# Lists' work one turn later, and the third segment product ahead of the third projection

## What is computed

```python
h = qw[input]                                         # table rounded per row
zxbcdt = layernorm(h) @ in_proj_w.T                   # 1030 columns: z, xBC, dt
xBC = silu(conv4(xBC) + conv_b); dt = softplus(dt + dt_bias)
y = ssd(x * dt, dt * A, B, C) + D * x                 # 6 heads, one chunk of 128
y = rms(y * silu(z)) * norm_w
h = h + sigmoid(gate1) * (y @ out_proj_w.T) + layernorm(h)
# experts on n = layernorm(h): 4 common, 4 unique, top 1 by softmax
common  = gelu(n @ W1c[e] + b1c[e]) @ W2c[e] + b2c[e]
dropped = rank of the token within its common expert >= 2048
out = h + common + dropped * unique
```

## Time and profile before

| | |
|---|---|
| median of 3 runs | 1068.1 us (1067.28 to 1074.15) |
| the profiled run, device time | 1069.56 us |
| its span, first to last instruction | 1067.8 us |
| TensorE busy | 922.9 us, 86% |
| VectorE busy | 678.0 us, 63% |
| ScalarE busy | 583.9 us, 55% |
| GpSimd busy | 531.8 us, 50% |
| sequence stage, convolution of turn 1 to that of turn 16 | 32 to 553 us |
| first unit's hidden product | 612.8 us |

### The profile page before, as it was taken

The page is one execution under the profiler, slowest core; times in us unless marked ns, Lnnn a source line. Parts: engine busy times, 40 slices in busy tenths (PEclk is TensorE's granted clock), DMA queues, the critical chain, the costliest instruction groups (busy, mean ns, idle before and its releaser), DMA issues.

```text
span 1067.8 us, 19889 instructions
## 1 busy us (share of the span) xinstructions
PE 922.9 (86%) x5743; PEld 600.0 (56%) x5744; DVE 678.0 (63%) x1999; ACT 583.9 (55%) x1196; POOL 531.8 (50%) x638
## 2 busy tenths in 40 slices
PE   0678899888988988899989788899988999999985
PEld 0233455455544554555455556677776676767774
DVE  3678999898898988989879614566671221212120
ACT  3657887787768877887685344323332323233330
POOL 6322436356354373561523517443437777775452
PEclk9899999999899999999898789999998999999997
DMA  4910011011101110110000122123431212222220
GB/s 111 319 51 9 16 46 44 4 47 46 46 3 45 46 48 1 47 46 31 3 31 31 49 62 80 49 80 116 139 88 45 70 49 66 56 62 74 69 58 22
DMA packets 50001, 61.54 MB, mean 58 GB/s; under 512 B 22524, under 2 KB 41688, under 8 KB 49412
## 3 DMA queue, kind: packets, MB, share of 16 engines
q0 software_dynamic: 16704, 30.54, 9.9%
q1 hardware_dynamic: 28580, 24.93, 7.7%
q10 hardware_dynamic: 4640, 5.13, 1.6%
HBM read 36.24 MB, written 25.92 MB: 58 GB/s over the span
## 4 chain that ended last, share of the span: by engine, by line
PE 39%; DVE 25%; ACT 13%; issue 12%; POOL 8%; DMA 2%; DVEq 0%; ACTq 0%; POOLq 0%
DVE xbc L1432 9%; PE cx L1217 6%; PE yb L1217 5%; PE mm L1205 4%; PE mm L1201 4%; PE mm L1055 4%; PE mm L1059 3%; PE sg L1201 3%; POOL list_c L537 3%; POOL list_u L573 2%; DVE mix L1452 2%; ACT rows_s L745 2%; DMA xg<-hr_dram,ids 2%; ACT h L692 2%; PE sg L973 2%
## 5 line engine op out<-in xcount | busy, mean ns | idle before, releaser
L1432 DVE SCALAR_TENSOR_TENSOR xbc<-mm,cw,xbc 128x508 f32<-128x508 f32 (+2 forms) x231 | 168.5, 740 | 32.0 <-ACT xbc L720 26.5
L1055 PE MATMUL mm<-xt_a,win_a 128*128 128x512 f32 x248 | 142.7, 658 | 36.5 <-DVE xbc L1432 27.1
L901 ACT ACTIVATE ht<-mm,b1s 128x256 f32<-128x256 f32 x102 | 44.7, 472 | 222.3 <-PE sg L1205 219.7
L512 POOL TENSOR_TENSOR ybuf<-ybuf,zs 128x384 f32<-128x384 f32 x64 | 68.7, 1073 | 108.7 <-DVE ybuf L1465 108.5
L589 POOL DMA_INDIRECT xg<-hr_dram,ids x80 | 81.1, 1013 | 80.5 <-DVE res L1759 44.8
L608 POOL DMA_INDIRECT out_dram<-osb,ids_s x80 | 82.3, 1028 | 64.2 <-DVE osb L1769 44.9
L720 ACT ACTIVATE xbc<-mm,cb,cw 128x512 f32<-128x512 f32 x77 | 56.6, 775 | 102.2 <-PE mm L1059 102.2
L1769 DVE TENSOR_TENSOR osb<-cx,res 128x192 f32<-128x192 f32 x40 | 14.2, 356 | 128.4 <-PE cx L1217 119.1
L1201 PE MATMUL mm<-fx_a,w1a_t 128*128 128x256 f32 x240 | 81.7, 423 | 13.7 <-issue 7.6
L1205 PE MATMUL mm<-fx_b,w1b_t 64*128 64x256 f32 x240 | 85.2, 436 | 0.0
L1205 PE MATMUL sg<-fx_b,w1b_t 64*128 64x256 f32 x240 | 85.2, 436 | 0.0
(11 more groups left out here) (275 smaller groups left out, 2051.2 us busy)
## 6 DMA issues: line engine op xcount, KB each, us to landing
hr_dram<-hr SPq DMA_DIRECT2D x16, 768.0 KB, 3.5
w2s<-in_w2c_dram SPq DMA_DIRECT2D x4, 576.0 KB, 8.6
w2s_u<-in_w2u_dram ACTq DMA_DIRECT2D x4, 576.0 KB
list_c<-fill SPq DMA_DIRECT2D x2, 1032.0 KB, 12.3
list_u<-fill SPq DMA_DIRECT2D x2, 1032.0 KB, 18.4
w1a<-in_w1c_dram SPq DMA_DIRECT2D x4, 384.0 KB, 7.1
w1a_u<-in_w1u_dram ACTq DMA_DIRECT2D x4, 384.0 KB
xg<-hr_dram,ids POOLq DMA_INDIRECT x80, 3.1
```

The costliest lines, as they stand in the source:

```text
L1055: mmul(tile_bank(g2, m)[:, :], win_a[:, column(m):column(m) + P], xt_a[:, p, :], start=True, stop=False)
L1432: ins = stt(out=dst_[:, :, back:L], in0=src[:, :, 0:L - back], scalar=cw[:, m, TAPS - 1 - back:TAPS - back], in1=dst_[:, :, back:L], op0=A ...
```

## The change

`list_tokens`, `prefixes` and `places` now work on `listed_turn(t)`, the batch of group t - 5, so they run in the following turn: prefixes behind `seg(1)` and ahead of `y(0)`, places behind VectorE's `y(0)`, and the list writes in two halves, the first behind `gate_y(0)`, the second behind `norm2`. The third segment product `seg(2)` stands ahead of `project(2)`. KNOWN is 5, not 6, and `early_units` stands at the end of turn 16. In turn 17 GpSimd gathers the first two units first of all, and the transposes, the copy and the weights of unit 0 are done within that turn. SyncE stores the group of turn 17 behind the first loads of unit numbers.

```diff
-KNOWN = 6
+KNOWN = 5
+def listed_turn(t):
+    g = t - 5 if t <= LAST_SSD else t - 4
+    return (batch(g), g) if 0 <= g < NG else (None, None)
 # SyncE, experts_sp
+            sp.wait_ge(s_mm, (XT + ZT) * NG)
             turn(0, 0, 0, body)
+            store(LAST_SSD, *groups(LAST_SSD))
             store(NG + 2, *groups(NG + 2))
 # GpSimd
-                def list_tokens():
+                def list_tokens(part=None):
...
-                    for j in range(GS * (g5 + 1 - first)):
+                    for j in range(n) if part is None else range(part * n // 2, (part + 1) * n // 2):
...
                 if t == LAST_SSD:
+                    for p in range(2):
+                        pool.wait_ge(s_st[p], CREDIT + 16 * (KNOWN - p))
+                    pool.wait_ge(s_mm, (XT + ZT) * NG)
+                    for v in range(2):
+                        gather_unit(0, 0, v, 0)
                     gate_y(0)
                     gate_y(1)
                     rms()
-                    for p in range(2):
-                        pool.wait_ge(s_st[p], CREDIT + 16 * (KNOWN - p))
-                    gather_unit(0, 0, 0, 0)
                     gate_y(2)
                     gate_y(3)
                     norm2()
-                    gather_unit(0, 0, 1, 0)
+                    list_tokens()
                     return
                 gate_y(0)
+                list_tokens(0)
                 rms()
...
                 norm2()
+                list_tokens(1)
                 gate_y(3)
-                list_tokens()
 # ScalarE, turn 17
                     copy_side()
+                    copy_x(0)
 # TensorE, turn 17
                     seg(1)
+                    prefixes()
                     cbx(1)
...
                     side_back()
+                    transpose_x(0, 0)
                     out_product(0)
 # TensorE, turns 1 to 16
                 seg(1)
+                prefixes()
                 y(0)
                 cbx(1)
+                seg(2)
 
                 project(2)
                 to_tp(g5, 2, 0)
                 project(3)
                 to_tp(g5, 2, 1)
-                seg(2)
                 y(1)
...
                 project(7)
                 y(3)
-                prefixes()
 # VectorE, turn 17
-                    early_units()
                     weights(0)
                     weights(1)
+                    places()
...
                     weights(3)
+                    dve.wait_ge(s_wc, n_w)
+                    dve.wait_ge(s_early, 1)
+                    unit_weights(0, 0, 0, 0)
                     residual(0)
 # VectorE, turns 1 to 16
                 y(0)
+                places()
...
                     clip(t + 1)
-                places()
+                if t + 1 == LAST_SSD:
+                    early_units()
```

More of the change, by code:

```diff
@@ L875, in body, with copy_x @@
                 sum_rows()
+            def copy_x(unit):
+                act.wait_ge(f_t, unit + 1)
+                nc.scalar.copy(fx_a[:, :], tp[:, 0:TL])
+                for n in range(2):
+                    last = nc.scalar.copy(fx_b[n * DB:(n + 1) * DB, :], tp[0:DB, TL:2 * TL])
+                last.then_inc(f_x, 1)
             rounded(0)
@@ L883, in _ @@
             before = [0]
-            def copy_x(unit):
-                act.wait_ge(f_t, unit + 1)
-                nc.scalar.copy(fx_a[:, :], tp[:, 0:TL])
-                for n in range(2):
-                    last = nc.scalar.copy(fx_b[n * DB:(n + 1) * DB, :], tp[0:DB, TL:2 * TL])
-                last.then_inc(f_x, 1)
             def gelus(m, i, v, unit):
```

69 lines of the change are left out of this document (34 added, 35 removed).

## The result

| | before | changed |
|---|---|---|
| median beside each other | 1071.12 us (1067.28 to 1076.56, 4 runs) | 1054.93 us (1053.1 to 1062.65, 4 runs) |
| ratio of the two | | 0.9855, 95% interval 0.9812 to 0.9897 |
| the same, measured again later | 1071.64 us (16 runs) | 1059.34 us (1053.63 to 1062.65, 6 runs), ratio 0.9878, 0.9838 to 0.9918 |
| span of the profiled execution | 1067.8 us | 1051.3 us |

The change makes the kernel 1.2 to 1.5% faster; the forecast was 1052, between 1045 and 1061. Where the 16.5 us of the two profiled executions lie can be read from the start of conv(0) in each turn: at the conv(0) of turn 5 the changed kernel is 1.9 us ahead, at that of turn 16 12.0 us, at the end 16.5. So turns 5 to 15 give 10.1 us (388.8 to 378.7), what stands ahead of turn 5 1.9, and all that stands behind turn 15 4.5.

The account below looks back on a forecast made before the run. GpSimd's list writes were taken to bound following turns, VectorE batch turns. Gains of 16.8 + 0.5 + 4.7 = 22.0 us, less 3 for the clock and 3 for hand-offs, left 16: 1068.1 - 16 = 1052, range 1045 to 1061.

Parts of the forecast that it names:

- Following turns held by norm1: Following turns: norm1 behind GpSimd's list writes holds project(5); without that a turn takes 33.3 us, 2.1 less than turn 11.
- Batch turns: VectorE bounds batch turns; places leaving takes 0.56 us off 35.30, and 34.8 us was taken.
- Front of a following turn: conv(0) to conv(2) takes 7.7 us, with project(3) 0.1 late and places fitting into VectorE's 0.66 us wait.
- Middle and end of the turn: Following turn: conv(2) to ScalarE's read of project(5) takes 6.7 us, from there to the next conv(0) 18.9.
- seg(2): Moving TensorE's seg(2) ahead of project(2) is worth nothing; bounds for a turn -0.5 to +0.3 us.
- The second half of the writes: Four GpSimd writes, 5.3 us, delay gate_y(3); covered by 1.9 us before squares, so they cost nothing.
- Turn 15: Turn 15 rounds no further group on ScalarE and takes about 31.5 us.
- Turns 5 to 15 as a sum: These turns fall from 388.8 to 372.0 us, a gain of 16.8, before 3 us put back for low-clock stretches.
- hand-offs: Some twenty hand-offs in the sum were rounded down by 0.15 us, so 3 us were put back.
- Ahead of turn 5: Turn 4 adds a gain of 0.5 us.
- The transition: Turn 17: unit 0's hidden product no longer waits for its weights; gain 4.7 us, bounds 3 to 5.2.
- rival (d): Clock falls between seg(1) and y(0) in each following turn; at 6 us a turn, 14 slower: 1082; chance 0.05.

Follow-up runs that it names:

- Experiment 1: Kernel before, with GpSimd's norm1 of the next group ahead of the eight list writes instead of behind them: 1067.95 us, ratio 0.9991.
- experiment 4: Changed kernel with the first four list writes ahead of gate_y(0) on GpSimd instead of behind it: 1050.09 us, ratio 0.982.
- experiment 5: Changed kernel with seg(2) back behind the second half of to_tp: 1055.08 us, ratio 0.9845.
- experiment 9: Changed kernel with all eight list writes behind norm2, none behind gate_y(0): 1073.89 us, ratio 0.9995.
- experiment 7: Changed kernel with turn 17's prefixes ahead of seg(0) instead of behind seg(1): 1057.59 us, ratio 0.9887.
- experiment 6: Changed kernel with the transition undone (both gathers, unit 0's transposes, copy and weights at their old places): 1057.4 us without one run of 4883, ratio 0.9898.
- experiment 3: Changed kernel with following turns' prefixes issued twice: 1084.88 us, ratio 1.0119; with three dense products instead of the second set: 1064.01 us, ratio 0.993.
- experiment 2: Kernel of experiment 1 plus two dense products in TensorE's idle time ahead of the prefixes in each batch turn: 1057.0 us, ratio 0.9874.
- experiment 8: Kernel of experiment 4 plus six dense products in TensorE's waits ahead of seg(0) and seg(1) in turn 17: 1048.81 us, ratio 0.9793.
- experiment 10: Kernel of experiment 8 with the last four VectorE operations of pick moved to the end of the following turn: 1052.58 us, ratio 0.9815.

## Why the prediction held, and where it did not

**Following turns held by norm1: right.** Experiment 1 shows it by itself: 33.6 us instead of 35.4.

**Batch turns: right.** 34.7, with 34.8 forecast.

**Front of a following turn: 7.7 forecast, 8.10 measured.** The term that was mis-sized is places: 0.56 us from the end of a batch turn, where nothing ran beside it, and 1.26 us at its new place beside gate_y(0). Both stood in the order shown ahead of the prediction, y(0) releasing gate_y(0) and places following y(0), and I priced places by its old row only. With this taken away (experiment 4) conv(2) stands at 7.65, so the walk of TensorE to project(3), 0.1 us late, was right. Middle and end of the turn, 6.7 and 18.9 forecast, are 6.77 and 18.95.

**seg(2): right**, nothing (experiment 5). **The second half of the writes: right** to cost nothing; the cover, 1.9 us by the forecast, is 1.6 (gate_y(3) ends at 402.99, the squares of turn 12 start at 404.59); the price without cover, "at most one per pair" for each us of excess, was right as a bound (2.4 us a pair for 3.4 us of excess, experiment 9).

**Turn 15: 31.5 forecast, 32.8 measured.** I took 1.8 us off for the group that ScalarE no longer rounds; from the read of project(5) to the next conv(0) it takes 17.88 us in both kernels, 1.0 less than elsewhere. The other 0.5 us is the front again.

**Turns 5 to 15 as a sum.** 372.0 forecast before what I put back, 378.7 measured. The 6.7 us: the low stretch in turn 13, 3.0; turn 15, 1.3; the front of turns 5, 7, 9, 11 and 13, 0.5 each, 2.5; turn 9 another 0.3; less 0.1 in each of five batch turns; that adds up to 6.6. I had put back 3 us for the clock and 3 for hand-offs. The first came out in size with one stretch of 3.0 where I thought of two of 1.4, and that is partly luck, since other executions of the same turns met up to four (experiment 7). The second was right by its sum only: hand-offs were not it.

**Ahead of turn 5: 0.5 forecast, 1.9 measured.** Turn 4 gave its 0.5 (34.97 to 34.42 us). The other 1.3 us are luck: four executions whose programs are the same up to there (the changed kernel twice, experiments 6 and 7) reach turn 5's conv(0) between 161.3 and 162.7 us.

**The transition: 4.7 forecast, 4.5 by the two spans, 4.1 by undoing it.** By the forecast the hidden product starts 55.9 us behind turn 16's conv(0); measured are 55.4. The transposes of hr gained 6.1 us instead of 4.7, because hr was ready at 602.06 and all of the hidden product ran at full clock; the upper bound of 5.2 was too low. Some of it is given back by the end. That the remaining 1.6 us go to the low stretch from 605.7 to 612.5, which falls on TensorE's side products and out_product there, is my reading and was not tested.

**The clock** was only a margin in the sum, and rival (d) at 0.05. The time shows that the margin was enough, but the mechanism is the largest thing that I underrated. The clock does fall behind the prefixes in following turns, in one turn of six in three executions (the changed kernel twice, experiment 6), in four of six in another (experiment 7), and from turn 7 on in every one with twice the products (experiment 3). Each of the stretches of 6.8 us costs 3.0 us, not the 6 that (d) took. It also decides what the change is worth: taking norm1's wait away in the old order changes the whole time by nothing (experiment 1), with the idle time ahead of the prefixes filled it gives 1057.0 (experiment 2). In the changed kernel the prefixes have a busy TensorE ahead of them; that this is a part of why it keeps its gain fits these two runs, but no run separates it from the change's other parts.

**What stays open:** why one execution of the same program meets one low stretch in turns 5 to 15 and another four, and why the three profiled executions with the list writes ahead of gate_y(0) (experiments 4, 8 and 10) met none, where all five with gate_y(0) first and the prefixes as changed (the changed kernel twice, experiments 5, 6 and 7) met at least one. The times differ with it: the executions of the changed kernel lie between 1053 and 1063.

**A better version.** Experiments 4 and 8, list writes ahead of gate_y(0) and TensorE's waits in turn 17 filled, give 1050.1 and 1048.8 us, ratios 0.982 and 0.9793. The interval of experiment 8 (0.9761 to 0.9826) lies below that of the changed kernel's second measurement (0.9838 to 0.9918) and overlaps a little with that of the first (0.9812 to 0.9897).

## What to carry over

Price a moved operation by what runs beside it at its new place, not only by its old row: 0.16 us became 0.82. When a wait is taken away and the time stays, look at the granted clock by turn before giving up the theory: the wait here was real, its 5.7 us in turns 5 to 15 were lost again behind turn 16's conv(0), and two dense products in the idle time ahead of each run of small ones were worth 11 us. In a pair of turns whose bounds differ, work moved from the full one to the other gains only as long as the other engine's row has slack.

## What was not expected of the hardware

- Eighteen products of 4 to 32 columns, 2.2 us, behind 1.11 us of idle TensorE were followed by low clock in three of the batch turns of experiment 1; with 1.4 us of dense products in that idle time, in none. Twice as many of them, with TensorE busy without a gap for 7 us ahead of the fall, brought 10.2 us at half clock in each of five following turns; one set with dense products of the second set's length brought one stretch in turns 5 to 15, away from the prefixes.
- Away from the prefixes the clock fell at the end of turn 7 of the kernel before, behind waits of 0.96 and 1.20 us less than 3 us apart; in its turns 5, 9, 11 and 13 it held behind the same two waits.
- A VectorE sum of 4 elements per partition waited for a GpSimd product of 384 elements to end, 0.82 us instead of 0.16. The convolution, which has one of its inputs in PSUM, was not stretched beside the same GpSimd operation (4.50 us for six in both cases).
- The list writes were not slowed at their new places: 0.95 to 1.09 us each, as in the earlier trace rows.
